# Attention: one matmul of turning Y back in each unit, and the copy of Y^T ahead of the high parts

## What is computed

```python
q = (xn @ q_w + q_b).reshape(Bx, Tx, H, -1)          # H = 16 heads of 32
k = (xn @ k_w + k_b).reshape(Bx, Tx, H, -1)
att = jnp.einsum('bnhl,bmhl->bnmh', q, k)
mask = src_mask.reshape(Bx, 1, Tx, 1)
att = att + (1.0 - mask) * -1000000.0
att = jax.nn.softmax(att, axis=2)
v = ((xn @ v_w + v_b) * src_mask[:, :, None]).reshape(Bx, Tx, H, -1)
y = jnp.einsum('bnmh,bmhl->bnhl', att, v).reshape(Bx, Tx, Dx)
```

## Time and profile before

| | us |
|---|---|
| median of three runs | 7927.27 (7926.64 to 7929.89) |
| the profiled execution | 7910.83, its span 7909.0 |
| attention stage in it | 570 to 1975 |

### The profile page before, as it was taken

How to read it: one execution, slowest core, us unless ns; L and a number is a source line. 1 busy time by engine, 2 the same in 40 slices (tenths; PEclk the granted TensorE clock), 3 DMA queues, 4 the chain that set the end, 5 groups by cost and what they waited for, 6 DMA issues and landing times. The chain is left out here.

```text
span 7909.0 us, 91399 instructions
## 1 busy us (share of the span) xinstructions
PE 6017.6 (76%) x31488; PEld 4106.9 (52%) x31488; DVE 5034.4 (64%) x6369; ACT 4519.9 (57%) x6695; POOL 2481.3 (31%) x1098
## 2 busy tenths in 40 slices
PE   4989999999559536899566666686899566666685
PEld 1448888888334333344355555543344355555542
DVE  2349999998321444454599999922354499999921
ACT  1128888888110231454599898812354599899920
POOL 0000000000000000000299999911000299999912
PEclk8999999999779768999799999998999799999997
DMA  5442223221542445333444544444333444554435
GB/s 198 193 156 60 70 62 78 60 70 45 215 162 95 156 157 193 138 151 133 148 130 130 144 133 129 124 127 136 138 152 139 140 129 129 142 137 129 128 100 178
DMA packets 614784, 1035.45 MB, mean 131 GB/s; under 512 B 104792, under 2 KB 252376, under 8 KB 607716
## 3 DMA queue, kind: packets, MB, share of 16 engines
q1 hardware_dynamic: 571812, 904.26, 36.9%
q10 hardware_dynamic: 37440, 109.20, 3.7%
q0 software_dynamic: 5120, 16.78, 0.6%
HBM read 640.74 MB, written 389.31 MB: 130 GB/s over the span
## 5 line engine op out<-in xcount | busy, mean ns | idle before, releaser
L1503 POOL TENSOR_TENSOR scan_hC<-scan_h,scan_Crep 128x1024 f32<-128x1024 f32 x1024 | 2394.7, 2365 | 3449.3 <-DVE scan_h L1630 3384.3
L1534 PE MATMUL scan_y<-ident,scan_hC 128*128 128x128 f32 x8192 | 1148.3, 285 | 826.6 <-POOL scan_hC L1503 826.4
L1534 PEld LDWEIGHTS scan_y<-ident,scan_hC 128*128 128x128 f32 x8192 | 908.7, 144 | 1025.7 <-POOL scan_hC L1503 890.5
L1594 ACT ACTIVATE scan_a<-scan_dt,scan_A 128x512 f32<-128x512 f32 x2048 | 1339.3, 690 | 26.4 <-DVE scan_h L1630 25.3
L1630 DVE TENSOR_TENSOR_SCAN scan_h<-scan_a,scan_carry,scan_h 128x512 f32<-128x512 f32 x1024 | 1212.2, 1260 | 42.0 <-issue 41.6
L1630 DVE TENSOR_TENSOR_SCAN scan_h<-scan_a,scan_h 128x512 f32<-128x512 f32 x1024 | 1160.8, 1202 | 96.2 <-ACT scan_a L1594 95.4
L1568 ACT COPY scan_h<-scan_drive 128x1024 f32<-128x1024 f32 x1024 | 1037.4, 1013 | 289.9 <-PE scan_drive L1522 254.6
L1522 PE MATMUL scan_drive<-scan_Bd,scan_dT 128*128 128x256 f32 x4096 | 751.6, 306 | 79.2 <-DMA scan_Bd<-scratch_Bcol 53.2
L834 DVE TENSOR_TENSOR att_pTlo<-att_TP,att_pThi 128x512 fp32r<-128x512 f32 x1024 | 657.9, 684 | 128.3 <-ACT att_pThi L872 126.4
L872 ACT CAST att_pThi<-att_TP 128x512 fp32r<-128x512 f32 x1024 | 548.2, 587 | 179.4 <-PE att_TP L767 172.4
L827 DVE CUSTOM_DVE_ANT_0 att_sm<-att_S,att_mneg 128x1024 f32<-128x1024 f32 x512 | 622.0, 1215 | 13.3 <-POOL att_mneg L745 13.0
(11 more groups left out here) (142 smaller groups left out, 6772.7 us busy)
## 6 DMA issues: line engine op xcount, KB each, us to landing
scan_dT<-scratch_dtuT SPq DMA_DIRECT2D x512, 256.0 KB, 6.1
scratch_dtuT<-ssmin_dT SPq DMA_DIRECT2D x128, 512.0 KB, 2.9
scan_Crep<-scratch_bc SPq DMA_DIRECT2D x64, 1024.0 KB, 12.6
scratch_xT<-n_xT ACTq DMA_DIRECT2D x24, 2048.0 KB, 6.3
p_xT<-scratch_xT SPq DMA_DIRECT2D x16, 2048.0 KB
att_q<-scratch_q_split SPq DMA_DIRECT2D x256, 128.0 KB, 3.0
att_k<-scratch_k_split SPq DMA_DIRECT2D x256, 128.0 KB, 3.2
scratch_uD<-ssmin_uD SPq DMA_DIRECT2D x64, 512.0 KB, 4.4
```

Source lines behind the costliest of these rows:

```text
L1503: nc.gpsimd.tensor_tensor(hC[k % 3][:], of, Crep[:, 2 * p:2 * p + 2, :], ALU.mult).then_inc(s["scaled"].handle, 1)
L1534: last = nc.tensor.matmul(y[j][:, t, :], hC[k % 3][:, i, t * P:(t + 1) * P], ident[:], start=(p == 0 and i == 0 and t == 0), stop=False, i ...
L1594: last = nc.scalar.activation(a[k % 2][:, i, :], dt[j][:], ACT.Exp, scale=A[:, m, 2 * p + i:2 * p + i + 1])
```

## The change

In `attention`:

- `yts` becomes a ring of two buffers. `copy_yt(g)` writes buffer g % 2 and waits for the `turn_back` of group g - 2 in place of g - 1.
- `turn_back` is called once for each unit, with one matmul in place of four, and increments `y_turned` each time. On PE it stands between `turn(u)` and `weigh(u - 2)`, for unit u - 7, in place of behind `weigh` in every fourth iteration.
- ACT issues `copy_yt` ahead of `copy_hi(u - 1)` in place of behind it.
- DVE, with u % 4 = 2, issues `shift(u + 2)` ahead of `take_lo(u - 1)`; `take` moves from u % 4 = 1, behind `shift`, to u % 4 = 3, between `take_lo` and `shift`, two iterations later.

```diff
-        yts = sb("yts", [2 * DH, 4, P])
+        yts = ring("yts", 2, [2 * DH, 4, P])
...
-            def turn_back(g):
-                w(pe, "yt_copied", g + 1)
-                if g >= 1:
-                    w(pe, "y_ready", g)
-                for n in range(4):
-                    last = nc.tensor.matmul(Y[:, n, :], yts[:, n, :], fold[:], start=True, stop=True)
-                last.then_inc(s["y_turned"].handle, 1)
+            def turn_back(u):
+                g = u // 4
+                if u % 4 == 0:
+                    w(pe, "yt_copied", g + 1)
+                    if g >= 1:
+                        w(pe, "y_ready", g)
+                nc.tensor.matmul(Y[:, u % 4, :], yts[g % 2][:, u % 4, :], fold[:], start=True, stop=True
+                                 ).then_inc(s["y_turned"].handle, 1)
...
                 turn(u)
+                if u >= 7:
+                    turn_back(u - 7)
                 if u >= 2:
                     weigh(u - 2)
-                if u >= 7 and u % 4 == 3:
-                    turn_back((u - 7) // 4)
...
-            turn_back(G - 1)
+            for u in range(U - 7, U):
+                turn_back(u)
...
-                w(dve, "y_turned", g + 1)
+                w(dve, "y_turned", 4 * g + 4)
...
+                if u % 4 == 2 and u + 2 < U:
+                    shift(u + 2)
                 if u >= 1:
                     take_lo(u - 1)
-                if u + 2 < U:
+                if u >= 11 and u % 4 == 3:
+                    take((u - 11) // 4)
+                if u % 4 != 2 and u + 2 < U:
                     shift(u + 2)
-                if u >= 9 and u % 4 == 1:
-                    take((u - 9) // 4)
...
-                if g >= 1:
-                    w(act, "y_turned", g)
-                nc.scalar.copy(yts[:], YT[:]).then_inc(s["yt_copied"].handle, 1)
+                if g >= 2:
+                    w(act, "y_turned", 4 * g - 4)
+                nc.scalar.copy(yts[g % 2][:], YT[:]).then_inc(s["yt_copied"].handle, 1)
...
+                if u >= 6 and u % 4 == 2:
+                    copy_yt((u - 6) // 4)
                 if u >= 1:
                     copy_hi(u - 1)
-                if u >= 6 and u % 4 == 2:
-                    copy_yt((u - 6) // 4)
```

## The result

The changed kernel takes 8209.35 us (median of 4, 8204.73 to 8211.26) against 7926.95 before: +282 us, a ratio of 1.0358 (95% interval 1.034 to 1.0376). The forecast was 8164, range 8038 to 8240: slower, as said, and 45 us more than said.

What follows compares the result with a forecast made beforehand. PE was taken to bound the kernel, with a loop in front of it. A group: 4 x 2.29 + 1.88 + 1.77 = 12.81 us against 10.93, +1.88, times 126 = +237; 7927 + 237 = 8164 us, range 8038 to 8240.

Steps and rivals of the forecast that it cites:

- Part 1, the excursion: On PE, `turn_back` in four pieces between `turn` and `weigh`: 0.47 us each, 1.88 a group against 1.18 before, +0.70.
- Part 2, the hold: ACT's `copy_yt` ahead of `copy_hi` makes PE stand 1.66 us before `turn(2)`; +1.18 us a group in all.
- The chain: From the start of `weigh` through copy of Y^T, `copy_hi` and `take_lo` to `turn(2)`: 3.14 us, PE filling 1.48.
- The 0.11 for the second half of `turn`: On PE, it waits for the second half of `take_lo`: 0.92 us instead of 0.81 from `turn` to `weigh`.
- Part 3: Second `yts` buffer costs 0, DVE's later `take` stays under PE's demand, single matmuls at the stage's end under 1 us.
- the main forecast: A wait of 1.66 us before `turn(2)` and c of 0.35 to 0.6: 8103 to 8230 us, chance 0.72.
- c: PE's cost per unit of one `turn_back` piece: 0.22 + 0.25 = 0.47 us, ends 0.22 and 0.62.
- the rival of the clock: PE's clock falls to 1.2 GHz for part of the attention stage: past 8240 us; chance 0.03 together with a longer hold.
- free switches: On PE, entering and leaving `turn_back` costs nothing, c = 0.22, the wait before `turn(2)` stands: 8038 us, chance 0.11.
- dear ones: On PE, entering and leaving `turn_back` costs as in the other stage, c = 0.62: 8240 us, chance 0.07.
- the hidden wait: ACT comes to the copy late anyway, so the wait before `turn(2)` adds only 0.11 us: 7955 us, chance 0.05.
- the faster case: PE loses its `turn_back` block, with cheap switches and no wait before `turn(2)`: -0.78 us a group, 7829 us, chance 0.02.

Runs made afterwards that it cites:

- the block at unit 2: The kernel before with the `turn_back` block of four behind `weigh` of unit 2 and `take` in DVE's unit 3 behind `shift`: 7848.6 us against 7913.3.
- the padded run: The changed kernel with the copy of Y^T back behind the high parts and `yts` and `fold` zero-padded to 128 rows: 7887.4 us against 7913.3 for the kernel before.

## Why the prediction was right, and where it was short

- **What bounds the kernel.** PE at 10.34 us of work and 0.59 of waits a group: borne out by the block at unit 2, where a group comes to 10.41.
- **Part 1, the excursion.** Forecast 0.47, measured 0.45 (2.74 against 2.29). Its make-up was off: 0.22 for two passes and 0.25 for the form in the text, 0.15 and 0.30 in the padded run. The passes come at 0.11 in a block of 64 rows, which is not what they cost between other matmuls of 128.
- **Part 2, the hold.** Forecast 1.66, measured 1.66, from a sum of four distances read from the trace of before. The chain came out at 3.10 for 3.14 and PE's own work beside it at 1.44 for 1.48. ACT's copy waited 2.30 where about 2.5 was said. The 0.11 for the second half of `turn` holds (`turn` to `turn_back` 1.09 against 0.97). Undoing it alone leaves 41 of the 282 us, so it takes back 241, of which the clock is a part.
- **Part 3.** The second buffer at nothing: measured 1.000. DVE's order inside the change at nothing: the run with the split undone is at +148 us, the copy alone at +155.
- **The sum.** 1.88 us a group forecast, 1.80 measured at full clock, 227 for 237 us. With the measured terms it would give 7927 + 227 = 8154, and the kernel takes 8209. That this lies inside the range, and even inside the 8103 to 8230 of the main forecast, is luck: that stretch was kept open for other values of c, and the clock filled it.
- **The step that failed** is the rival of the clock. It was named, with its mechanism, and given 0.03 together with a longer hold, on the strength of the scan stage's 0.98 at a lower busy share. It came about in part: the granted clock of the stage was 0.96. That cost some 62 us in the profiled execution; by the medians it is 55, the 45 by which the forecast is short and the 10 by which the group's sum was long. The busy share was the wrong thing to compare: the clock was up at 88% in two of the runs and down at 89% in the changed kernel. The text had the gaps of the excursions and the gap of the hold in its own sum and didn't ask what they do together.
- **The other rivals** all fall: free switches (0.22) and dear ones (0.62) by the excursion of 0.45, the hidden wait and the faster case by the idle 1.50 before `turn` in every group.

What remains open is why the clock falls. The runs show that neither the hold nor the split does it alone, and that it stays up with the padded form, with the shorter hold, and, but for two windows, with either neighbour of the hold rid of its excursion. Whether the place of the excursions, their number or the length of the group decides isn't told apart, nor why most holds have no fall behind them.

## What to carry to other kernels

Before moving an instruction ahead of another on an in-order engine, look for who issues what it waits for: if that stands behind an instruction which in turn needs what you have now pushed back, the engines stop in a ring for the length of the whole chain, less what each can still do meanwhile, and the chain can be added up from distances between starts in the old trace. Here work in a block was cheaper than the same work spread out, because each piece took the array from 128 rows to 64 and back; spread it only if a gap takes it in, and place the block where PE waits anyway. Padding a small contraction to 128 rows with zeros can be faster than leaving it at 64.

## What the runs showed of the hardware

- A 64-row matmul between matmuls of 128 rows costs 0.30 us to enter and leave; with 128 rows, half of them zeros, its two passes of 32 columns cost 0.15 us in place of 0.45. With four such places a group the padding was worth 67 us here (7887.4 against 7954.7), less than the 151 of PE's own work.
- TensorE's granted clock fell to 1.2 GHz 38 times in the stage of the changed kernel, 130 us together, with PE busy 89% of 600 to 1900 us and no idle time before a held `turn` above 1.50 us; 37 of the falls began 1.4 to 2.0 us after the start of a held `turn`. It stayed at 2.4 GHz in that stretch with the hold alone (8067.9 us), with the split alone (7954.7 us), with the padded form (8012.0 us) and with the hold at 1.13 us (8112.4 us).
